# Gate row of the last expert layer: from the last sum into the sends of the expert blocks

## The reference, cut to what matters

```python
def _L1_ffn_ref(x, norm_weight, gate_w, w1, b1, w2, b2):   # 8 experts, 2 of them per token
    t = x * jax.lax.rsqrt(jnp.mean(x * x, axis=-1, keepdims=True) + RMS_EPS) * norm_weight
    tokens = t.reshape(-1, D)
    gate_scores, expert_idx = jax.lax.top_k(tokens @ gate_w.T, TOP_K)
    routing_weights = jax.nn.softmax(gate_scores, axis=-1)
    combine = jnp.zeros((T, E), tokens.dtype).at[jnp.arange(T)[:, None], expert_idx].add(routing_weights)
    def body(acc, params):
        W1, B1, W2, B2, c = params
        h = jax.nn.gelu(tokens @ W1.T + B1, approximate=False)
        o = h @ W2.T + B2
        return (acc + c[:, None] * o, None)
    out, _ = jax.lax.scan(body, jnp.zeros_like(tokens), (w1, b1, w2, b2, combine.T))
    return x + out.reshape(B, S, D)
...
h = _layernorm(x, axis=-1) * (1 + cb) + sb
x = x + gb * _L1_ffn_ref(h, ...)
```

## Time and profile before

| | us |
|---|---|
| median of the runs (lowest, highest) | 2220.2 (2217.27, 2221.49) |
| profiled execution, from first to last instruction | 2098.1 |
| median less that span | 122.1 |
| block loop of layer D, per block | 6.31 |
| last scatter issued | 2045.4 |
| first instruction of the last sum | 2053.5 |
| last add | 2093.2 |

### The profile page before, as it was taken

One profiled execution on the slowest core, in us unless ns is written; L12 is line 12 of the kernel. 1 busy time (PEld: TensorE's weight loads), 2 busy tenths in 40 slices (PEclk: granted clock), 3 DMA queues, 4 the chain that ended last, 5 costly groups with the idle time before them and its releaser, 6 DMA issues. The chain is left out here.

```text
span 2098.1 us, 31683 instructions
## 1 busy us (share of the span) xinstructions
PE 1780.8 (85%) x11154; PEld 1568.2 (75%) x11154; DVE 1419.9 (68%) x2513; ACT 1049.2 (50%) x2094; POOL 918.1 (44%) x948
## 2 busy tenths in 40 slices
PE   3799999999988999999949999995579884899990
PEld 1788888888877888887748888874256673899990
DVE  4555565556433888776656987764898587688877
ACT  4243344334412344654455355543788553788872
POOL 0222232233211114777720257774555240788845
PEclk7899999999988999999969999998789965899995
DMA  6000000000023131666654136664500013687847
GB/s 210 1 1 11 10 0 10 10 10 0 10 79 106 61 114 32 200 197 183 176 163 141 59 108 197 199 171 159 181 19 1 1 61 111 208 277 269 266 160 245
DMA packets 145940, 231.62 MB, mean 110 GB/s; under 512 B 28050, under 2 KB 103060, under 8 KB 140820
## 3 DMA queue, kind: packets, MB, share of 16 engines
q1 hardware_dynamic: 122196, 165.47, 24.1%
q0 software_dynamic: 23616, 64.52, 10.6%
HBM read 174.07 MB, written 55.33 MB: 109 GB/s over the span
## 5 line engine op out<-in xcount | busy, mean ns | idle before, releaser
L160 POOL TENSOR_TENSOR spare_g<-neg_half 128x1 f32<-128x1 f32 x96 | 28.9, 301 | 594.2 <-ACT a_sg L509 138.8
L149 PE MATMUL bank<-gT_hi,w_hi 128*128 128x512 f32 x592 | 246.3, 416 | 2.4 <-DVE gT_lo L1422 2.4
L149 PE MATMUL bank<-gT_hi,w_lo 128*128 128x512 f32 x592 | 237.7, 402 | 0.0
L149 PE MATMUL bank<-gT_lo,w_hi 128*128 128x512 f32 x592 | 236.6, 400 | 0.0
L1634 POOL DMA_INDIRECT b_kept<-sent,b_scatter_i x168 | 176.7, 1052 | 62.8 <-issue 48.4
L1627 POOL DMA_INDIRECT got<-b_rows,b_gather_i x168 | 170.8, 1016 | 65.1 <-issue 50.0
L1422 DVE TENSOR_TENSOR gT_lo<-bank,gT_hi 128x512 fp32r<-128x512 f32 x148 | 97.1, 689 | 92.8 <-ACT gT_hi L1235 57.5
L1260 ACT ACTIVATE m_hi<-gs 128x512 fp32r<-128x512 f32 x116 | 72.9, 633 | 173.2 <-DVE gs L1429 115.1
L149 PE MATMUL bank<-w_hi,m_hi 128*128 128x256 f32 x464 | 132.6, 286 | 14.6 <-DVE sent L1451 14.4
L149 PEld LDWEIGHTS bank<-gT_hi,w_lo 128*128 128x128 f32 x592 | 113.3, 191 | 27.6
L149 PE MATMUL bank<-w_lo,m_hi 128*128 128x256 f32 x464 | 131.7, 284 | 0.0
(11 more groups left out here) (454 smaller groups left out, 5780.0 us busy)
## 6 DMA issues: line engine op xcount, KB each, us to landing
v_raw<-in_units SPq DMA_DIRECT2D x39, 1024.0 KB, 5.0
w_raw<-in_units SPq DMA_DIRECT2D x92, 256.0 KB, 3.2
w_raw<-b_folded SPq DMA_DIRECT2D x44, 256.0 KB, 3.7
b_rows<-x SPq DMA_DIRECT2D x16, 512.0 KB, 2.9
got<-b_rows SPq DMA_DIRECT2D x16, 512.0 KB, 3.9
close_back<-b_kept SPq DMA_DIRECT2D x16, 512.0 KB, 7.9
d_back<-d_kept SPq DMA_DIRECT2D x16, 512.0 KB, 5.2
got<-b_kept SPq DMA_DIRECT2D x12, 512.0 KB, 5.5
```

What stands on the lines that cost most here:

```text
L149: ins = pe.matmul(out, a, b, start=first and n == 0, stop=last and n == of - 1)
L160: eng.tensor_tensor(b.spare_g[:, i:i + 1], b.neg_half[:, 0:1], b.neg_half[:, 0:1], ALU.mult)
```

## The change

- `d_vector`'s `send` gets a second instruction: after its add has finished, VectorE multiplies `sent` (128x512) by the gate row. The scatters wait for this (`sent`) and not for the add (`o`).
- The GpSimd part of the last sum (`d_combine_gpsimd`) is gone.
- The last sum adds a whole tile, 1024 columns, in one VectorE instruction, after the tile's four mixes.
- `back` has seven buffers in place of four, and each tile its own semaphore for the loads.

```diff
+TAIL_BUFS = 7
...
 def d_combine_sync(sp, b, s, r, kept, out):
...
     for t in range(NB):
-        if t >= 4:
-            sp.wait_ge(r.summed.sem, r.summed.at(t - 4))
+        if t >= TAIL_BUFS:
+            sp.wait_ge(r.summed.sem, r.summed.at(t - TAIL_BUFS))
         for i in range(PICKS):
-            sp.dma_start(b.back[t % 4][:, i, :, :], kept[...]...).then_inc(r.fetched[t % 4].sem, 16)
+            sp.dma_start(b.back[t % TAIL_BUFS][:, i, :, :], kept[...]...).then_inc(r.fetched[t].sem, 16)
...
     def scatters(k):
-        g.wait_ge(r.o.sem, r.o.at(k))
+        g.wait_ge(r.sent.sem, r.sent.at(k))
...
     def send(k):
...
         v.tensor_tensor(b.sent[k % 4][:, :, :], d_banks(b, k)[1][:, :].rearrange("p (c n) -> p c n", c=QBD), mid(b.w_b2[k % 6], QBD), ALU.add).then_inc(r.o.sem, 1)
+        v.wait_ge(r.o.sem, r.o.at(k))
+        v.tensor_tensor(b.sent[k % 4][:, :, :], b.sent[k % 4][:, :, :], mid(b.mod[:, GB, :], QBD), ALU.mult).then_inc(r.sent.sem, 1)
...
 def d_combine_vector(v, b, r):
     for t in range(NB):
-        back = b.back[t % 4]
+        back = b.back[t % TAIL_BUFS]
         for c in range(CT):
             v.wait_ge(r.weighed.sem, r.weighed.at(t, c + 1))
             v.scalar_tensor_tensor(back[:, 0, c, :], back[:, 1, c, :], b.r_gb[:, t * CT + c:t * CT + c + 1], back[:, 0, c, :], ALU.mult, ALU.add).then_inc(r.mixed.sem, 1)
-        for c in range(CT):
-            v.wait_ge(r.gated.sem, r.gated.at(t, c + 1))
-            xt = b.x[:, (t * CT + c) * D:(t * CT + c + 1) * D]
-            v.tensor_tensor(xt, xt, back[:, 0, c, :], ALU.add).then_inc(r.summed.sem, 1)
-
-
-def d_combine_gpsimd(g, b, r):
-    for t in range(NB):
-        for c in range(CT):
-            g.wait_ge(r.mixed.sem, r.mixed.at(t, c + 1))
-            g.tensor_tensor(b.back[t % 4][:, 0, c, :], b.back[t % 4][:, 0, c, :], b.mod[:, GB, :], ALU.mult).then_inc(r.gated.sem, 1)
-
+        v.wait_ge(r.mixed.sem, r.mixed.at(t))
+        xt = tile_of(b, t)
+        v.tensor_tensor(xt, xt, flat(back[:, 0, :, :]), ALU.add).then_inc(r.summed.sem, 1)
```

More of the change, by code:

```diff
@@ L2279, in d_combine_sync @@
     for t in range(NB):
-        if t >= 4:
-            sp.wait_ge(r.summed.sem, r.summed.at(t - 4))
+        if t >= TAIL_BUFS:
+            sp.wait_ge(r.summed.sem, r.summed.at(t - TAIL_BUFS))
         for i in range(PICKS):
-            sp.dma_start(b.back[t % 4][:, i, :, :], kept[i * N + t * TB:i * N + (t + 1) * TB, :].rearrange("(c p) n -> p c n", p=P)).then_inc(r.fetched[t % 4].sem, 16)
+            sp.dma_start(b.back[t % TAIL_BUFS][:, i, :, :], kept[i * N + t * TB:i * N + (t + 1) * TB, :].rearrange("(c p) n -> p c n", p=P)).then_inc(r.fetched[t].sem, 16)
     for t in range(NB):
@@ L2477, in d_combine_scalar @@
     for t in range(NB):
-        act.wait_ge(r.fetched[t % 4].sem, r.fetched[t % 4].at(t // 4))
+        back = b.back[t % TAIL_BUFS]
+        act.wait_ge(r.fetched[t].sem, r.fetched[t].at(0))
         for c in range(CT):
-            act.activation(b.back[t % 4][:, 0, c, :], b.back[t % 4][:, 0, c, :], ACT.Copy, scale=b.r_ga[:, t * CT + c:t * CT + c + 1]).then_inc(r.weighed.sem, 1)
+            act.activation(back[:, 0, c, :], back[:, 0, c, :], ACT.Copy, scale=b.r_ga[:, t * CT + c:t * CT + c + 1]).then_inc(r.weighed.sem, 1)
 def d_combine_vector(v, b, r):
     for t in range(NB):
-        back = b.back[t % 4]
+        back = b.back[t % TAIL_BUFS]
         for c in range(CT):
@@ L2674, in program @@
             with ExitStack() as e:
-                b.back = [sb(e, f"d_back{i}", [P, PICKS, CT, D]) for i in range(4)]
+                b.back = [sb(e, f"d_back{i}", [P, PICKS, CT, D]) for i in range(TAIL_BUFS)]
             bD = Names(b)
@@ L2793, in program @@
                        gT_lo=("gT_lo", KD), w1_hi=("wg_hi", 1), w1_lo=("wg_lo", 1), w2_hi=("wd_hi", 1), w2_lo=("wd_lo", 1), up_ps=("up_ps", 2), m=("m", KH), m_hi=("m_hi", 2),
-                       m_lo=("m_lo", 2), down_ps=("down_ps", 1), o=("o", 1), weighed=("bias_folded", CT), mixed=("gate_ps", CT), gated=("sg", CT), summed=("x", CT))
+                       m_lo=("m_lo", 2), down_ps=("down_ps", 1), o=("o", 1), weighed=("bias_folded", CT), mixed=("gate_ps", CT), sent=("sg", 1), summed=("x", 1))
         rd = Names(**{name: after_b(old, per) for name, (old, per) in d_table.items()})
@@ L2798, in program @@
         rd.loaded = [rb.closing[4 + i].again(1) for i in range(4)]
-        rd.fetched = [rb.closing[i].again(1, 16 * PICKS) for i in range(4)]
+        rd.fetched = [rb.closing[i].again(1, 16 * PICKS) for i in range(4)] + [s.load_c[i].again(1, 16 * PICKS) for i in range(4)]
         rd.gathered = [rb.gathered[i].again(uses_of(2 * NBB, 4, i), 16 * GROUP * QBD) for i in range(4)] + [signal(f"d_gathered{i}", 16 * GROUP * QBD) for i in range(4, 6)]
@@ L2813, in gpsimd_d @@
             d_gpsimd(g, bD, rd, rows, kept)
-            d_combine_gpsimd(g, bD, rd)
         def scalar_d(act):
```

## The result

The changed kernel takes 2266.98 us in the median of 4 runs (2250.93 to 2272.78), the kernel before 2219.54 (4 runs, 2217.27 to 2221.49). The ratio is 1.0214, with a 95% interval of 1.0176 to 1.0252: **slower**, where 2210.4 had been forecast. The profiled execution spans 2270.9 us.

A forecast was written before the change was run, and what follows sets the result against it. VectorE was taken to bound the last stage (39.4 us), TensorE to set the block loop's pace. Tail -10.5, last multiply +0.7, loop 0 gave -9.8 us: 2210.4 us from 2220.2, range 2206.5 to 2216.

The forecast's parts named there:

- The sum forecast: Whole kernel: tail -10.5 us, last multiply +0.7, block loop 0, together -9.8 us.
- GpSimd's queue: Block loop: the multiply turns a 0.46 us hold into 0.04, four issues still fit into 6.31 us; cost nothing.
- The sum for the loop: Block loop: the added multiply and GpSimd's issues together cost 0, blocks staying at 6.31 us.
- Rival 3: Block loop: multiply delays GpSimd's queue 0.69 us a block, +9 net, 2229 us; chance 0.06, middle ground 0.08.
- The multiply in the block: VectorE in the block loop: 39 multiplies near 685 ns, hidden beside TensorE, the shift gone within each block; cost nothing.
- the last block: End of the loop: no cover there, so the scatter and everything behind it move 0.7 us later.
- The tail: Last sum: VectorE needs 2.92 us a tile instead of 4.92, traffic ends last; -10.5 us before the last multiply's +0.7.
- The stores' 10.9 us: End of the tail: eight stores of 0.524 MB at 385 GB/s move after all loads, 2.1 us behind the last byte.
- The base: Profiled span 2098.1 us against a 2220.2 median: the 122.1 difference was put on the forecast span of 2088.3.

The follow-up runs named there:

- e1: The kernel before, run and profiled again word for word: 2220.01 us, ratio 0.9998.
- e12: e9 with more tiny GpSimd pauses, after every second gather of groups 5 to 9 and the scatters of blocks 0 to 9: 2220.62 us, ratio 0.9976.
- e2: The changed kernel, run and profiled once more: 2268.12 us, ratio 1.0202 against the kernel before.
- e10: The kernel before with the send's add made twice, the second also reading PSUM, and no multiply: 2273.04 us, ratio 1.0239.
- e6: The changed kernel with the same multiply moved behind the next block's first weight remainder on VectorE: 2213.15 us, ratio 0.9959 against the kernel before.
- e3: The changed kernel's multiply in the send, last sum without GpSimd but with four buffers and four adds a tile: 2253.5 us, ratio 1.0155.
- e4: The kernel before with only seven buffers and one add a tile; GpSimd still multiplies by the gate row: 2219.67 us, ratio 0.9999.
- e8: The kernel before with three tiny GpSimd instructions after each gather of groups 1 to 6 in layer D: 2236.43 us, ratio 1.0064.
- e7: The changed kernel with two gathers and two scatters per block instead of four and four per two blocks: 2212.4 us, ratio 0.9959 against the kernel before.
- e11: The changed kernel with tiny GpSimd pauses after every second gather from the seventh group and after scatter pairs: 2217.48 us, ratio 0.9967 against the kernel before.
- e9: e6 with gathers four groups ahead instead of six and two tiny GpSimd instructions after each gather of groups 1 to 4: 2199.2 us, ratio 0.992.

## Why the prediction was wrong

**Sign and size of the whole.** Against e1's profile the changed one adds up: 8.9 us before D (code that the change doesn't touch; D starts anywhere from 1884.8 to 1901.2 in the profiles of e1 to e12 and the change), -1.3 at D's start, +56.4 in the loop, -11.6 in the tail, together the 52.4 between the spans (47.4 between the medians of the timed runs). The sum forecast was -9.8.

**The step that failed** is GpSimd's queue: "The hold of 0.46 us turns into one of 0.04, and the four issues still fit into 6.31. I cost this at nothing." The hold did vanish, and in e2's run the other one with it. But I read holds only as a cost, to be hidden or not, and not as what made GpSimd's pace equal to the block's. The sum for the loop was 0 and the loop measured +56.4. Without the holds the queue runs ahead, collects waits (129.2 us) and issues in runs of eight at 1.29 us, at whose ends the others stand still or wait for one another. I asked what is late when GpSimd is later, never what happens when it is earlier.

I cited the Trainium skill, GPSIMD Engine Reference, Key points, for GpSimd's contention with VectorE instructions of two SBUF inputs. The traces agree on the hold (1.70 and 1.41 us against 0.94 to 1.00 in e1), but the loss is not that contention: e10 has it with an added instruction of one SBUF input, and e6 has no loss with the multiply in full.

**Rival 3** had the engine and the sign right, at 0.06, and the mechanism the wrong way round: it let the queue be delayed by 0.69 us a block and VectorE wait for send buffers. The queue is less busy, and GpSimd waits for VectorE. That it named a slower end is luck: the mechanism that it gave did not occur. It also counted 32 blocks beside gathers; in the traces they are 26 to 27.

**The multiply in the block** was costed rightly on VectorE. VectorE of e2 in order of time:

```profile
2055.12 0.68 DVE L2457 TENSOR_TENSOR d_sent<-bank,v_b 128x512 f32<-128x512 f32 x1
2055.84 0.69 DVE L2459 TENSOR_TENSOR d_sent<-d_sent,mod 128x512 f32<-128x512 f32 x1
2056.45 1.22 DVE L2442 TENSOR_TENSOR v_lo<-v_raw,v_hi 128x1024 fp32r<-128x1024 f32 x1
```

It takes 0.69 us and shifts the remainder by as much, as written; and e6 shows that VectorE has room for 39 of them at 6.31 us a block. What I wrote of the last block holds too: the first pair is taken up 11.0 us after the last send (2238.51 - 2227.51), before 10.3 (2053.50 - 2043.17), 0.7 more.

**The tail** was right in its mechanism, and its term too small: -11.5 (43.4 - 54.9) for the forecast -9.8, both with the last multiply in it. The mixes, the add, the pairs' distance (3.04 for 3.01) and the rates are as written. The stores' 10.9 us were counted from the moment at which ScalarE takes up the last pair (2259.81), but DMA moves at the stores' rate from 2259 on, since bytes stop before the landing is seen; and behind the last byte (some 2269.6, by the 197 GB/s of the last stretch shown) lie 1.3 us, where I had 2.1. From 2259.81 to the end it is 11.1, and I had 13.0. Of the three edits only GpSimd's removal pays (e3 43.6, e4 55.6).

**The base.** A profile that lies 122 us from the median is a warning. I called the difference time around the span, and it lies inside. At D's start, 36.4 us in e1 against 15.0, it is a standstill beside indirect transfers, as e8 shows, and that is 21.4 us of the 120. Whether the 97.4 us before D have the same cause, no run here tests. Had I asked where 122 us can be, the queue would have had more than 6 in 100.

**Stays open.** What is shown is that the pace of GpSimd's issues decides over the loss: e6 takes it away, e7 and e11 all but some 7 us of it, and e10 makes it without the multiply. Which resource is blocked is not shown. It isn't the bytes alone: DMA moves 130 and 172 GB/s in the mean of 1900 to 1910 and 1910 to 1920 us, while e1 stands still at D's start, and though it reaches 401 from 1910 to 1912, TensorE stands as still at 86 (1904 to 1906); and in e1's loop DMA is busy at 0.95 or more in 55 of the 140 stretches of one microsecond from 1950 to 2090, and TensorE has no break in any. The distance between issues and the number of transfers under way change together in every run here, so either may be what counts. Nor is it shown why the given profile has gathers 1.25 us apart at D's start and no standstill: density alone is not enough. e9 and e12 leave open whether a pace exists that keeps the short start and meets no run later; 2199.2 us is the best measured.

## What to carry to other kernels

An engine that is slowed by contention may be paced by it: before moving work that holds a queue back, ask what the queue does when it is free, and whether its issues will come in runs. Where several engines idle at once with nothing shown that they wait for, look at the spacing of the indirect transfers, and test it with tiny instructions between them; where those make the queue late, the buffers behind it wait (e8) or the run comes later (e12). And compare the profile's span with the timed runs before building on its stages.

## What the runs showed of the hardware that was not expected

- Runs of indirect transfers issued 1.25 to 1.29 us apart go with TensorE, ScalarE and VectorE standing still, 9.74 us at once in e12 and 14.91 in e1; at a mean distance of 1.58 us (6.31 / 4, e1's loop) or 1.74 and more (e9's start) they don't. The given profile has such a run at D's start without standstill.
- Adding instructions to GpSimd's queue made the kernel faster: e11 against the change, 2217.48 to 2266.98 us in the medians.
- A full DMA does not stop TensorE by itself: e1's loop has DMA busy at 0.95 or more in 55 of 140 microseconds and TensorE at 50.00 of 50.
- In a tail with GpSimd and VectorE both on two-input work, 32 mixes of 256 columns take 712 ns each beside multiplies of 855 (e4), and 1.67 us per four without GpSimd (changed kernel).
